# Inverse roots of the second expert route, in a fused transformer kernel's MLP stage: a Newton iteration on VectorE in place of GpSimd's power

## The reference

```
_layernorm(x) = (x - mean(x)) / sqrt(var(x) + 1e-5)
expert layer, on that:
  xn = (x - mean(x)) * rsqrt(var(x) + 1e-5) * gamma + beta
  probs = softmax(xn @ Wr + br); scores, idx = top_k(probs, 2)
  output = sum over the 2 experts of score * (expert(xn) ...); x + output
```

## Time and profile before

| what | value |
|---|---|
| median of 3 runs | 1336.76 us (1336.28 to 1343.72) |
| the profiled execution's time | 1339.15 us |
| its span | 1336.8 us |
| busy share of the span: PE, DVE, ACT, POOL | 90%, 68%, 62%, 38% |
| mean granted TensorE clock | 0.958 of full |
| x_add of row 0 to x_add of row 7 (L2143) | 1039.66 to 1136.57 us |

### The profile page before, as it was taken

One profiled execution on the slowest core, in us unless ns is written; L12 is line 12 of the kernel. 1 busy time (PEld: TensorE's weight loads), 2 busy tenths in 40 slices (PEclk: granted clock), 3 DMA queues, 4 the chain that ended last, 5 costly groups with the idle time before them and its releaser, 6 DMA issues. The chain is left out here.

```text
span 1336.8 us, 26862 instructions
## 1 busy us (share of the span) xinstructions
PE 1201.7 (90%) x7787; PEld 913.1 (68%) x7787; DVE 914.6 (68%) x3538; ACT 829.8 (62%) x2478; POOL 505.1 (38%) x619
## 2 busy tenths in 40 slices
PE   6999999999999998699975999999996989199990
PEld 4766676666667665499963777777774656199990
DVE  6788888888888775444436888888873666244445
ACT  5898888888989885244432565566554666044440
POOL 2111324142424232455542343433432376545550
PEclk9999999999999999799997999999997999599995
DMA  9100000000000000222221000000000011222226
GB/s 294 49 2 1 12 7 11 7 13 8 16 5 13 8 11 5 80 67 71 71 77 41 17 16 17 16 1 1 1 1 1 13 40 40 79 61 71 70 73 195
DMA packets 54443, 52.91 MB, mean 40 GB/s; under 512 B 7341, under 2 KB 43098, under 8 KB 54330
## 3 DMA queue, kind: packets, MB, share of 16 engines
q1 hardware_dynamic: 36320, 29.39, 7.7%
q0 software_dynamic: 8928, 17.84, 4.0%
q10 hardware_dynamic: 9082, 4.33, 1.1%
HBM read 29.48 MB, written 22.05 MB: 39 GB/s over the span
## 5 line engine op out<-in xcount | busy, mean ns | idle before, releaser
L1356 ACT ACTIVATE prob<-prob,negmax 128x256 f32<-128x256 f32 (+3 forms) x512 | 283.2, 556 | 37.5 <-DVE negmax L1450 37.5
L1450 DVE CUSTOM_DVE_ANT_0 prob<-bank,mask 128x256 f32<-128x256 f32 (+3 forms) x512 | 224.6, 480 | 36.8 <-PE bank L1166 34.4
L1529 POOL TENSOR_TENSOR Vs<-Vh_sb,rinv 128x512 f32<-128x512 f32 x64 | 66.7, 1042 | 355.9 <-DVE rinv L1428 355.9
L1052 POOL DMA_INDIRECT expert_out<-f_x_yb,f_x_to x142 | 136.8, 963 | 153.4 <-DVE f_x_yb L1040 131.0
L1178 PE MATMUL bank<-prob,Vs 128*64 128x512 f32 (+3 forms) x1024 | 153.6, 443 | 2.9 <-POOL Vs L1529 2.8
L680 POOL DMA_INDIRECT expert_in<-f_xn,f_slot x128 | 126.4, 987 | 46.2 <-issue 30.8
L984 PE MATMUL bank<-f_x_xbT,W_sb 128*128 128x256 f32 x568 | 138.6, 388 | 1.6 <-DVE f_x_xbT L1020 1.5
L1005 ACT ACTIVATE f_x_hid<-bank,cols 128x256 f32<-128x256 f32 x144 | 63.8, 475 | 91.4 <-PE bank L984 91.4
L984 PEld LDWEIGHTS bank<-f_x_xbT,W_sb 128*128 128x128 f32 x568 | 104.6, 194 | 14.8 <-DVE f_x_xbT L1020 2.6
L1178 PEld LDWEIGHTS bank<-prob,Vs 128*64 128x64 f32 x1024 | 64.2, 137 | 72.7 <-issue 62.9
L1005 ACT ACTIVATE prob<-bank,cols 128x256 f32<-128x256 f32 x140 | 62.1, 474 | 82.8 <-PE bank L984 82.8
(11 more groups left out here) (263 smaller groups left out, 3169.1 us busy)
## 6 DMA issues: line engine op xcount, KB each, us to landing
f_x_xb<-expert_in SPq DMA_DIRECT2D x73, 130.0 KB, 2.2
b_crows<-expert_out SPq DMA_DIRECT2D x16, 256.0 KB, 2.8
c_crows<-expert_out SPq DMA_DIRECT2D x16, 256.0 KB, 4.2
expert_out<-f_x_yb,f_x_to POOLq DMA_INDIRECT x142
expert_in<-fill ACTq DMA_DIRECT2D x16, 130.0 KB, 3.6
x_sb<-in_L_attn_a_x_dram SPq DMA_DIRECT2D x8, 256.0 KB, 6.4
W_sb<-in_L_ffn_W_dram SPq DMA_DIRECT2D x1, 2048.0 KB, 10.0
expert_in<-f_xn,f_slot POOLq DMA_INDIRECT x128, 2.4
```

The lines of the kernel that those rows point to most:

```text
L1052: pool.indirect_dma_start(yg, bass.IndirectOffsetOnAxis(ap=self.to[:, t:t + 1], axis=0), self.yb[:, t, :], None).then_inc(self.stored[t], 16)
L1356: nc.scalar.activation(mine, mine, ACT.Exp, scale=-1.0, bias=negmax[:, g % 2, i, a:a + 1], accum_out=rowsum[:, g % 2, i, a:a + 1]).then_in ...
L1450: nc.vector.tensor_tensor_reduce(out=prob[:, g % 2, a, columns(i)], in0=score_bank(i, a), in1=mask[:, T - width[i]:], scale=-1.0, scalar=H ...
```

## The change

In the route of mlp_stage the two inverse roots of a row are made by VectorE, in a new function dve_power which route_stats calls right behind dve_base, so ahead of gated(b, 0). A first guess comes from the bits of the base taken as an integer (a shift by one, then a constant minus that), and three Newton rounds follow, of three instructions each. These are eleven instructions on 128x8 elements, each of which waits for the one before it. The last raises rstd, and one more semaphore increment closes the count. pool_power and its two calls in GpSimd's program are gone. Of the start-up increments, those of rstd go from GpSimd to VectorE.

```diff
--- before.py
+++ after.py
@@ -307,8 +307,14 @@
                 self.of_dve = (self.stats, self.moments, self.xn, self.y, self.lo_ready)
                 if lean:
                     self.base, self.terms = sem(name + "_base_ready", at), sem(name + "_terms_ready", at)
-                    self.of_dve = (self.stats, self.moments, self.xn, self.base, self.terms)
-                self.of_pool = (self.pool_step, self.rstd, *[s for s in (self.sum, self.htok) if s is not None])
+                    self.rooted = sem(name + "_root_step", at)
+                    self.root = sb(name + "_root", [P, 2, 2, NT], at=at)
+                    self.root_square = sb(name + "_root_square", [P, 2, NT], at=at)
+                    self.root_error = sb(name + "_root_error", [P, 2, NT], at=at)
+                    self.root_bits = sb(name + "_root_bits", [P, 2, NT], i32, at=at)
+                    self.of_dve = (self.stats, self.moments, self.xn, self.base, self.terms, self.rstd, self.rooted)
+                self.of_pool = () if lean else (
+                    self.pool_step, self.rstd, *[s for s in (self.sum, self.htok) if s is not None])
 
             def tiles(self, b, where=None):
                 return (self.src if where is None else where)[:, bass.ds(b * NT, NT), :]
@@ -360,11 +366,35 @@
                 nc.vector.tensor_scalar(self.power[:, u, 3, :], var, 1.0 + EPS, EPS * EPS, ALU.mult,
                                         ALU.add).then_inc(self.base, 1)
 
-            def pool_power(self, pool, b, u):
-                pool.wait_ge(self.base, START + 2 * b + 2)
-                nc.gpsimd.tensor_tensor(self.power[:, u, 4:6, :], self.power[:, u, 2:4, :],
-                                        half[:, :].unsqueeze(1).to_broadcast([P, 2, NT]),
-                                        ALU.pow).then_inc(self.rstd, 1)
+            ROUNDS = 3
+            ROOT_STEPS = 2 + 3 * ROUNDS
+
+            def dve_power(self, dve, b, u):
+
+                base = self.power[:, u, 2:4, :]
+                y = [self.root[:, k, :, :] for k in range(2)]
+                step = START + b * self.ROOT_STEPS
+                dve.wait_ge(self.base, START + 2 * b + 2)
+                nc.vector.tensor_scalar(self.root_bits[:, :, :], base.bitcast(i32), 1, None,
+                                        ALU.logical_shift_right).then_inc(self.rooted, 1)
+                dve.wait_ge(self.rooted, step + 1)
+                nc.vector.tensor_scalar(y[0].bitcast(i32), self.root_bits[:, :, :], -1.0, float(0x5F3759DF),
+                                        ALU.mult, ALU.add).then_inc(self.rooted, 1)
+                for r in range(self.ROUNDS):
+                    done = step + 2 + 3 * r
+                    out = self.power[:, u, 4:6, :] if r == self.ROUNDS - 1 else y[(r + 1) % 2]
+                    dve.wait_ge(self.rooted, done)
+                    nc.vector.tensor_tensor(self.root_square[:, :, :], y[r % 2], y[r % 2],
+                                            ALU.mult).then_inc(self.rooted, 1)
+                    dve.wait_ge(self.rooted, done + 1)
+                    nc.vector.scalar_tensor_tensor(out=self.root_error[:, :, :], in0=self.root_square[:, :, :],
+                                                   scalar=-0.5, in1=base, op0=ALU.mult,
+                                                   op1=ALU.mult).then_inc(self.rooted, 1)
+                    dve.wait_ge(self.rooted, done + 2)
+                    ins = nc.vector.scalar_tensor_tensor(out=out, in0=self.root_error[:, :, :], scalar=1.5, in1=y[r % 2],
+                                                         op0=ALU.add, op1=ALU.mult)
+                    ins.then_inc(self.rooted if r < self.ROUNDS - 1 else self.rstd, 1)
+                dve.sem_inc(self.rooted, 1)
 
             def dve_terms(self, dve, b, u):
                 dve.wait_ge(self.rstd, START + b + 1)
@@ -2149,6 +2179,7 @@
                             dve.sem_inc(x_complete, 1)
                             route.norm.dve_stats(dve, b, slot_of(b))
                             route.norm.dve_base(dve, b, slot_of(b))
+                            route.norm.dve_power(dve, b, slot_of(b))
 
                         def route_normalise(b):
                             route.dve_normalise(dve, b, slot_of(b))
@@ -2209,10 +2240,8 @@
                         pool.wait_ge(z_squares, 1)
                         pool_z_rstd(pool, LAST, z_mean, 1).then_inc(last_rstd, 1)
                         for b in range(1, B):
-                            route.norm.pool_power(pool, b - 1, slot_of(b - 1))
                             if b >= 2:
                                 scatter_in_halves(b - 2, slot_of(b - 2))
-                        route.norm.pool_power(pool, LAST, slot_of(LAST))
                         route.pool_scatter(pool, LAST - 1, slot_of(LAST - 1))
                         route.pool_scatter(pool, LAST, slot_of(LAST))
                         experts.pool_work(pool, experts.load_counts(pool))
```

## The result

The changed kernel takes 1351.28 us (median of 4 runs, 1350.08 to 1353.89) against 1337.09 us (4 runs, 1336.28 to 1343.72): a ratio of 1.0094, with a 95% interval from 1.0070 to 1.0118. It is slower by 14.2 us, and the forecast of 1350.3 was 1.0 us under it. Whether that is more than one per cent the interval leaves open, as the even chances had it. Its profiled execution took 1351.41 us with a span of 1349.7; the spans differ by 12.9.

The account below looks back on a forecast made before the run. VectorE's path up to normalising was taken to set each row. Seven rows' 15.75 us, less 2.60 of GpSimd waits, plus 0.42 in row 7, gave 13.57 on 1336.76: 1350.3 us, own range 1346 to 1355, stated finally as 1344 to 1356.

Parts of the forecast that it names:

- the even chances: Whole kernel: chance 0.50 of slower by more than one per cent, 0.49 of within one per cent, 0.01 of faster.
- What sets the row: In the loop, VectorE up to normalising sets the row; anything added between x_add and normalising lengthens it by as much.
- Eleven steps of 0.20 us: VectorE's chain between bases and gated products: eleven dependent steps at 0.20 us, 2.20 us a row.
- The bounds, 0.08 and 0.31: Step spacing in VectorE's chain: 0.08 us without waits, 0.88 in all; 0.31 if half stretch beside scatters, 3.4 us.
- The closing increment: Semaphore increment ending VectorE's chain: 0.11 us, of which 0.05 counted, making 2.25 us a row.
- What GpSimd's going gives back: Normalising no longer waits for GpSimd: rows 0, 2, 4 and 6 give back 2.60 us together.
- row 7: The last row, without MLP work to cover the power: normalising starts 0.42 us later.
- GpSimd's queue at nothing: GpSimd's earlier scatters and freed 1.67 us a row count at nothing, since VectorE's slots set the last scatter.
- (1): VectorE's chain runs at the pace of instructions that don't wait: 0.93 us a row, 1339.8 us; chance 0.06.
- (2): The chain is hidden in VectorE's idle time, TensorE always having other work: 1334.6 us, not slower; chance 0.05.
- (3): TensorE's clock falls in the loop's new gaps: 1360 us for one row, 1420 for all seven; chance 0.04.
- (4): GpSimd's scatter stretches VectorE's chain to 3.4 us a row: 1359.6 us; chance 0.05.

Follow-up runs that it names:

- power_sooner: The kernel before, with GpSimd's power of a row issued ahead of the last of eight scatters instead of behind it: 1337.57 us, ratio 0.9981.
- both_paths: The kernel before, GpSimd's power kept and used, plus the same eleven dependent instructions and increment on VectorE, result unused: 1353.91 us, ratio 1.0114.
- eleven_apart: The kernel before, GpSimd's power kept and used, plus eleven VectorE instructions that each read only the base, results unused: 1344.11 us, ratio 1.0039.
- chain_late: The changed kernel with the chain moved behind the gated products and slots, right ahead of normalising: 1361.66 us, ratio 1.0179.
- woven: The changed kernel with the chain's steps spread over gated products and slots, without the closing increment: 1347.13 us, ratio 1.0066.

## Why the prediction was right, point by point

*What sets the row.* Right. L459 waits for normalising in the rows after as L429 did before, and what is put on VectorE ahead of normalising makes the row longer: nine steps fewer and nine more change the mean row by -1.80 and (at a clock of 1.00) +1.75 us, and the chain costs the same ahead of the gated products and behind the slots.

*Eleven steps of 0.20 us.* Right as counted from one pair of instructions, L929 and L931; shift, guess and Newton steps on 8 elements take the same 0.17 us and 0.03 of wait. One of the 88 lines took 0.37. The bounds, 0.08 and 0.31, were not needed; the lower one was met by instructions that don't wait on one another.

*The closing increment.* Mis-sized: I counted 0.05 of its 0.11 us, the gated product starts 0.20 us behind the eleventh instruction instead of 0.07, so nothing of it was hidden. A row pays 2.35, not 2.25, seven rows 16.45 and with the one long line 16.64, not 15.75.

*What GpSimd's going gives back.* Mis-sized the other way. The seven rows grew by 13.04 us, so 16.64 - 13.04 = 3.60 came back, not 2.60. Row 2 gave 1.37, row 4 0.67, row 6 0.32 (forecast 1.36, 0.49 and 0.49), rows 1, 3 and 5 together 0.21; row 0 gave 1.03 in place of 0.26. There I had TensorE late next; in the changed profile its transposes in row 0 start 0.06 us behind normalising, and the gated pair takes 1.29 us instead of 1.47, because it no longer waits for its second up matmul; 0.32 us lie ahead of the chain, in the statistics. They are not chance: in row 0 VectorE idles there for 0.20 us in the kernel before and in power_sooner and for 0.50 in both_paths and eleven_apart, which all keep GpSimd's power, and in no kernel without it; why stays open. The two wrong sizes, 0.89 too little and 1.00 too little, nearly cancel: 13.04 + 0.46 for row 7 (forecast 0.42) is 13.5, the sum 13.57. The mechanism was right, but that the forecast came within 1.0 us is in part luck.

*GpSimd's queue at nothing.* Right: the last scatter waits for VectorE, and both_paths, which keeps the power on GpSimd, isn't faster or slower for it beyond the intervals.

*The rivals.* (1) fell by the spacing, and eleven_apart shows about what it would have been, with GpSimd's power kept: 1344. (2) fell, since the wait before L429 is in every row. (3), the clock, didn't happen in the changed kernel's profile, but I gave the wrong reason for its safety: 1.9 us without TensorE in a row had kept the clock, and I took the new gap to be of that kind. The changed kernel has up to 2.7 us in two pieces and kept it; chain_late has as much in one piece and lost it in six of seven rows. But both_paths, with two pieces like the changed kernel's, lost it in two rows, so nothing here shows that the changed kernel keeps it in every execution. (4) hardly happened: 87 of the chain's 88 lines keep their 0.17 us beside scatters, and the long one cost 0.19 us.

## What to carry to other kernels

An operation of 1.7 us on an idle engine is cheaper than 2.4 us on the engine that sets the row, however small its instructions are; ask first where its waits come from, which here was the order of GpSimd's queue, and change that. A chain of small dependent instructions is priced by steps, at the spacing of a dependent pair of the same size in the trace; put other work of the engine between its steps, and it costs a quarter less (some 0.6 of 2.35 us a row here, 0.78 with the closing increment gone too). A gap that is opened on TensorE can cost more than its length, by the clock behind it: read the granted clock of every row in the changed profile, as the gap's length alone did not tell it here.

## What the runs showed of the hardware that was not expected

The granted clock left 1.00 behind one gap of 2.7 us in an otherwise busy row (chain_late: 1.00 through the gap, 0.54 from 1061.20 to 1064.50, most of it at 1.2 GHz, and 0.96 from there to 1070.00), and stayed at 1.00 in the changed kernel with gaps of 1.8 and 0.95 us in a row. Two matmuls without use in that gap made the kernel 9 us faster. The length of the gap alone doesn't tell what the clock will do: in woven it stayed at 1.00 behind single gaps of up to 2.31 us, and in both_paths, whose TensorE program is that of the changed kernel, it fell in two rows, in one of them behind a gap of 1.75. What else decides is open, and so is how often the changed kernel loses it.

A semaphore increment as an instruction of its own, on VectorE behind a short instruction, delays the next by 0.11 us where the instruction before had itself waited (0.20 with it, 0.09 without), which is half a step of the chain. In eleven_apart, where none of the eleven waits for another, the same increment delays nothing: the gated product follows at 0.08.
